# Where the nine sums of a source are written: PSUM layout, 16-bit words and GpSimd's copy in a graph kernel

## The chip, the cores and the metric

One core of one Trainium2 chip. The metric is the device time of one execution in microseconds; the kernel before takes 516.81 us (median of 3 runs, 516.4 to 516.84).

## The reference

6250 nodes with 64 features, 200,000 edges sorted by target, two graph convolutions behind a layer norm and a residual:

```python
def _ngcf_conv(x, W1, W2, src, dst, n_nodes):
    ones = jnp.ones(src.shape[0], dtype=x.dtype)
    deg_out = jnp.clip(jax.ops.segment_sum(ones, src, num_segments=n_nodes), 1.0)
    deg_in = jnp.clip(jax.ops.segment_sum(ones, dst, num_segments=n_nodes), 1.0)
    norm = jax.lax.rsqrt(deg_out[src] * deg_in[dst])
    h_src = x[src]
    h_dst = x[dst]
    msg = (h_src @ W1 + h_src * h_dst @ W2) * norm[:, None]
    agg = jax.ops.segment_sum(msg, dst, num_segments=n_nodes)
    return x @ W1 + agg

h = jnp.maximum(_layernorm(x, axis=-1), 0.0)
h1 = jax.nn.relu(_ngcf_conv(h, W1_1, W2_1, src, dst, n))
x = x + _ngcf_conv(h1, W1_2, W2_2, src, dst, n)
```

(n_nodes in the layer is 12500, but only the 6250 rows that occur are computed.)

## The kernel before

The kernel turns the edge list into a dense matrix of edge counts (targets by sources) on the chip, and then does both layers as dense matmuls with it. `fast_path` does all of it; a `general_path` behind it runs only where a flag says that the counts do not fit, which these inputs never need.

*Building the words.* Targets come in 49 blocks of 128, and each block in two units of 64 (98 units, `UNITS`). For a block VectorE writes one-hot rows `los` (`low_hots`, L663, a ring of three blocks), for a pair of steps TensorE multiplies `select` with the edges' digits into `diff` (`weigh_hots`, L879) and ScalarE turns that into weights `hots` (`save_weights`, L1025). Then `products(u)` (L895) runs 24 accumulated matmuls of 98 columns into one PSUM bank, `slab[u % 2]`. A bank holds nine rows of 49 sums: row 0 is the count of edges by source (for the out-degree), rows 1 to 8 are packed words, each with counts of eight targets in 2-bit fields. Each matmul adds 49 columns to row 0 and 49 columns to row `group + 1`.

*Saving them.* ScalarE's `save_words(u)` (L1034) copies the 441 sums to `saved` (a ring of two blocks), with 2^23 added so that the integer stands in the low bits. GpSimd's `keep_words(b)`, once per block, adds the histogram rows of both units to `hist` (L460) and copies the low 16 bits of the word rows, transposed, to `words[:, b]` (L463), 16 words for each of the 49 sources. The copy releases ScalarE's ring (`words_copied`) and VectorE's unpack of that block. GpSimd runs in order, and the same queue holds the indirect fetches of the edges, the decoding of later tiles (`decode`) and the layer norm (`moments`, `apply_norm`).

*Unpacking.* `unpack(n)` (L702 for the first field, L704 for the other three) takes the 400 32-bit words of a block and writes four fields as 8-bit floats, one block of the adjacency matrix, into one of five homes. Blocks 0, 1 and 2 are unpacked beside the building, behind the `los` of blocks 30, 34 and 38 (`UNPACK_BESIDE`), later ones three positions ahead of their use.

*The join.* After the last block VectorE adds the two histogram halves (L729) and the last block's two histogram rows out of PSUM (L732, L735), takes the root's reciprocal and scales h into `parts0` (L746, L753) in pieces, with which TensorE begins layer 1 (L966).

*The layers.* 98 positions (`POSITIONS`), 49 for each layer. Position n has 49 matmuls (L988), one per source block; between them, at fixed places, the transposition of a position before (`turn_pair`, L937, at q = 26, waits for VectorE's pair L781 and GpSimd's product L551) and its weight matmul (`weigh`, L955 or L959, at q = 43). VectorE's order in a position of layer 2 is: finish (L802), sums (L774), pair (L781), unpack (L702, L704 three times). The flag is made at position BLOCKS + 4 from two totals.

Of the kernel before, what the change touches and what calls it, by code (L numbers as in the profile page):

```python
# [19 lines left out]
P, Q = 125, 50  # L20
# [24 lines left out]
HOT_RING = 4  # L45
SAVED_RING = 2
EARLY_TILES = 4
# [4 lines left out]
BOTH = 1.0 + 0x3C / 1024.0  # L52
MAGIC = 2.0 ** 23
SC0 = 2.0 ** 12
# [58 lines left out]
def fast_path(nc, c, x, src, dst, weights, out, flag):  # L113
    def sb(name, shape, dt):
        return c.enter_context(nc.sbuf_tensor(name, shape, dt))
# [11 lines left out]

    words = sb("words", [128, BLOCKS, Q, WORDS], U16)
    x_sb = sb("x_sb", [128, BLOCKS, D], FP32)
# [3 lines left out]
    hots = sb("hots", [128, HOT_RING, USTEPS, Q - 1], FP16)  # L133
    saved = sb("saved", [128, SAVED_RING, 2, COLS], FP32)
    mixed = sb("mixed", [128, KEYLEN + STACKLEN], BF16)
# [9 lines left out]
    mask = sb("mask", [96, WORDS], FP32)  # L145
    hist = sb("hist", [128, 2, Q - 1], I32)
    last = sb("last", [SROWS, 1], FP32)
# [28 lines left out]
    rdo_sc0 = sb("rdo_sc0", [128, BLOCKS], FP32)  # L176
    totals = sb("totals", [128, 2], FP32)
    checks = sb("checks", [1, 2], FP32)
# [17 lines left out]
    junk = los_1[0:ROWS, 3 * GROUPS + 2 * WINDOW:3 * GROUPS + 2 * WINDOW + TILES * SAMPLES].rearrange("p (t e) -> p t e", t=TILES)  # L196
    words_late = flat_words[:, (BLOCKS - 3) * Q * WORDS:].bitcast(FP32)
    wabs = words_late[:, 448:512]
# [68 lines left out]
    weights_ready = sem("weights_ready")  # L267
    words_copied = sem("words_copied")
    hist_added = sem("hist_added")
# [103 lines left out]
    with nc.Block() as block:  # L373
# [52 lines left out]
        def _(pool):  # L426
# [19 lines left out]
                                    base=0, pattern=[[-1, 128]], channel_multiplier=1).then_inc(consts, 1)  # L446
            nc.gpsimd.memset(hist[:].bitcast(FP32), -(2.0 ** 97)).then_inc(hist_added, 1)
            nc.gpsimd.memset(words[:, :, Q - 1:Q, :], 0).then_inc(consts, 1)
# [5 lines left out]

            def keep_words(b):
                pool.wait_ge(slab_saved, 2 * b + 2)
                both = saved[:, b % SAVED_RING]
                if b < BLOCKS - 1:
                    pool.wait_ge(hist_added, b + 1)
                    nc.gpsimd.tensor_tensor(out=hist[:], in0=hist[:], in1=both[:, :, 0:Q - 1].bitcast(I32),  # L460
                                            op=ALU.add).then_inc(hist_added, 1)
                low = both[:, :, Q - 1:COLS].bitcast(U16).rearrange("p i (w q k) -> p q i w k", w=8, k=2)
                nc.gpsimd.tensor_scalar(words[:, b, 0:Q - 1, :].rearrange("p q (i w) -> p q i w", i=2), low[:, :, :, :, 0],  # L463
                                        1.0, 0.0, ALU.mult, ALU.add).then_inc(words_copied, 1)

# [62 lines left out]
            for u in range(UNITS):  # L528
                if u % 2 == 1:
                    keep_words(u // 2)  # L530
# [47 lines left out]
        def _(dve):  # L578
# [113 lines left out]
            def unpack(n, fields=range(4)):  # L692
                if n >= 5:
                    dve.wait_ge(acc_ready, n - 2)
                if n < BLOCKS:
                    dve.wait_ge(words_copied, n + 1)
                packed = words[:, n % BLOCKS].rearrange("p q w -> p (q w)").bitcast(I32).rearrange(
                    "p (q w) -> p q w", w=WORDS // 2)
                for s in fields:
                    to = tile_words[home(n)][:, :, 8 * s:8 * s + 8]  # L700
# [27 lines left out]
            dve.wait_ge(hist_added, BLOCKS)  # L728
            nc.vector.tensor_tensor(out=rdo[:], in0=hist[:, 0], in1=hist[:, 1], op=ALU.add).then_inc(deg_summed, 1)  # L729
            dve.wait_ge(deg_summed, 1)  # L730
            dve.wait_ge(slab_ready, UNITS - 1)
            nc.vector.tensor_tensor(out=degrees, in0=rdo[:], in1=slab[0][:, 0:Q - 1], op=ALU.add).then_inc(deg_summed, 1)  # L732
            dve.wait_ge(deg_summed, 2)
            dve.wait_ge(slab_ready, UNITS)
            nc.vector.tensor_tensor(out=degrees, in0=degrees, in1=slab[1][:, 0:Q - 1], op=ALU.add).then_inc(deg_summed, 1)  # L735
            dve.wait_ge(deg_summed, 3)
# [88 lines left out]
            for n in range(TOGETHER + 1, POSITIONS + 1):  # L825
                finish(n - 1)
                if n == BLOCKS:
                    dve.wait_ge(root_ready, BLOCKS)
                    nc.vector.tensor_reduce(out=totals[:, 1:2], in_=deg_in[:], axis=AX.X,
                                            op=ALU.add).then_inc(totals_ready, 1)  # L830
                if n == BLOCKS + 4:
                    dve.wait_ge(totals_summed, 1)
                    v(nc.vector.tensor_scalar(checks[:], sum_ps[0:1, 0:2], float(EDGES), None, ALU.is_equal))
                    v(nc.vector.tensor_tensor(out=flag[:], in0=checks[:, 0:1], in1=checks[:, 1:2], op=ALU.mult))
                if n < POSITIONS:
                    if n >= BLOCKS:
                        dve.wait_ge(z_used, min(n - BLOCKS + 1, BLOCKS))
                    sums(n)
                    if n + 3 < POSITIONS:
                        unpack(n + 3, (0, 1))  # L840
                    if n < BLOCKS:
                        low_turned(n)
                    if n + 3 < POSITIONS:
                        unpack(n + 3, (2, 3))

        @block.tensor
        def _(pe):
# [36 lines left out]
            def products(u):  # L884
# [86 lines left out]
            for n in range(TOGETHER, POSITIONS):  # L971
# [7 lines left out]
                for q in range(BLOCKS):  # L979
# [24 lines left out]
        def _(act):  # L1004
# [458 lines left out]
```

## Time and profile before

| | |
|---|---|
| median of the runs | 516.81 us |
| profiled execution, its own time | 518.48 us |
| its span | 516.8 us |
| TensorE busy | 485.1 us, 94% |
| VectorE busy | 410.2 us, 79% |
| ScalarE busy | 252.4 us, 49% |
| GpSimd busy | 220.9 us, 43% |

The span is what the profiler's records cover; the execution's own time is 1.7 us longer. Busy shares are averages over stages: about 25 us of start, the building of the words to 200 us, then two layers.

### The profile page before, as it was taken

How to read it: one execution, taken by the hardware profiler on the slowest of the kernel's cores; microseconds unless marked ns; L12 is line 12 of the kernel's file. 1: busy time of each engine (PE TensorE's matmuls, PEld its weight loads, DVE VectorE, ACT ScalarE, POOL GpSimd, SP SyncE). 2: the span in 40 equal slices, each digit the busy share in tenths (PEclk: the TensorE clock that was granted, in tenths of full speed). 3: DMA queues.
4: the chain of work that ended last, by engine and by line, in shares of the span. 5: the costliest groups of instructions: out<-in, count | busy, mean ns of one | idle time of the engine just before them, and what ended most of it. 6: DMA issues, size and time to landing. Idle time of an engine off the chain costs nothing.

```text
span 516.8 us, 19829 instructions
## 1 busy us (share of the span) xinstructions
PE 485.1 (94%) x7949; PEld 455.4 (88%) x7949; DVE 410.2 (79%) x1040; ACT 252.4 (49%) x726; POOL 220.9 (43%) x425
## 2 busy tenths in 40 slices
PE   2699999989997997999999999999999999999995
PEld 2577788878786887999999999999999999999995
DVE  6978999999999986987777777776766666666662
ACT  0279999999998795433333333333111121112111
POOL 3336879788999483453333433333100001100000
PEclk9879999999999898999999999999999999999998
DMA  2257102020201000000000000000000110020011
GB/s 68 82 95 94 47 21 64 3 63 3 65 1 43 2 3 1 3 4 2 3 4 3 3 3 2 3 4 3 3 1 3 21 26 1 3 44 1 3 29 20
DMA packets 17912, 10.89 MB, mean 21 GB/s; under 512 B 14144, under 2 KB 16496, under 8 KB 17821
## 3 DMA queue, kind: packets, MB, share of 16 engines
q1 hardware_dynamic: 17117, 7.60, 7.7%
q0 software_dynamic: 672, 2.01, 1.4%
q8 instruction: 64, 1.05, 0.8%
q14 instruction: 27, 0.22, 0.1%
q10 hardware_dynamic: 32, 0.01, 0.0%
HBM read 6.21 MB, written 3.33 MB: 18 GB/s over the span
## 4 chain that ended last, share of the span: by engine, by line
PE 72%; DVE 17%; issue 5%; ACT 2%; DMA 2%; POOL 1%; SPq 0%; DVEq 0%; ACTq 0%; POOLq 0%
PE diff L988 34%; PE iota_bank L988 17%; DVE los L663 9%; PE slab L895 8%; PE diff L879 4%; PE diff L959 2%; PE diff L966 1%; DVE stats L671 1%; ACT hots L1025 1%; PE slab L937 1%; DMA los<-in_dst_dram 1%; PE diff L955 1%; PE turn_t L937 1%; DVE rows L652 1%; DVE late L704 1%
## 5 line engine op out<-in xcount | busy, mean ns | idle before, releaser
L663 DVE TENSOR_TENSOR los<-mixed,iota_bank 128x5120 bf16<-128x5120 bf16 x49 | 136.3, 2810 | 7.0 <-PE slab L895 6.9
L895 PEld LDWEIGHTS slab<-hots,los 128*128 128x128 bf16 x2352 | 122.0, 99 | 17.5 <-issue 4.4
L895 PE MATMUL slab<-hots,los 128*128 128x98 fp8e5 x2352 | 128.2, 211 | 3.0 <-DVE los L663 2.9
L551 POOL TENSOR_TENSOR work<-work,h 128x64 f32<-128x64 f32 x98 | 31.4, 321 | 214.7 <-DVE work L774 214.7
L1025 ACT ACTIVATE hots<-diff 128x784 f16<-128x784 f32 x147 | 118.7, 847 | 9.1 <-PE diff L879 8.8
L988 PE MATMUL diff<-late,mixed 128*128 128x128 f16 x1616 | 104.4, 219 | 0.0
L988 PEld LDWEIGHTS diff<-late,mixed 128*128 128x128 fp8e4 x1616 | 98.7, 99 | 0.4
L988 PE MATMUL diff<-los,mixed 128*128 128x129 f16 x1470 | 95.7, 220 | 0.0
L988 PEld LDWEIGHTS diff<-los,mixed 128*128 128x128 fp8e4 x1470 | 89.3, 98 | 0.3
L463 POOL TENSOR_SCALAR words<-saved 128x784 uint16<-128x784 uint16 x49 | 79.2, 1617 | 7.8 <-ACT saved L1034 7.4
L879 PE MATMUL diff<-select,mixed 80*128 80x392 f16 x294 | 69.4, 342 | 8.4 <-ACT hots L1025 5.0
L704 DVE TENSOR_SCALAR mixed<-words 128x400 int32<-128x400 int32 x192 | 61.1, 359 | 0.0
L1034 ACT ACTIVATE saved<-slab 128x441 f32<-128x441 f32 x98 | 53.4, 545 | 10.6 <-PE slab L895 7.1
L988 PE MATMUL iota_bank<-late,tile 128*128 128x128 f16 x784 | 51.5, 219 | 0.0
L988 PE MATMUL iota_bank<-los,tile 128*128 128x129 f16 x735 | 49.0, 220 | 0.0
L988 PEld LDWEIGHTS iota_bank<-late,tile 128*128 128x128 fp8e4 x784 | 48.0, 98 | 0.2
L988 PEld LDWEIGHTS iota_bank<-los,tile 128*128 128x128 fp8e4 x735 | 45.0, 98 | 0.2
L781 DVE SCALAR_TENSOR_TENSOR work<-h,stats,work 128x64 f32<-128x64 f32 x98 | 39.5, 403 | 4.5
L879 PEld LDWEIGHTS diff<-select,mixed 80*128 80x128 f16 x294 | 23.6, 101 | 20.3 <-ACT hots L1025 10.2
L802 DVE SCALAR_TENSOR_TENSOR x_sb<-diff,stats,x_sb 128x64 f32<-128x64 f32 x49 | 13.9, 284 | 30.5 <-PE diff L959 30.5
L460 POOL TENSOR_TENSOR hist<-hist,saved 128x98 int32<-128x98 int32 x48 | 18.6, 387 | 39.6 <-ACT saved L1034 31.4
L704 DVE TENSOR_SCALAR tile<-words 128x400 int32<-128x400 int32 x96 | 32.7, 380 | 0.0
(172 smaller groups left out, 537.8 us busy)
## 6 DMA issues: line engine op xcount, KB each, us to landing
x_sb<-in_x_dram SPq DMA_DIRECT2D x4, 384.0 KB
rows_table<-rows SPq DMA_DIRECT2D x6, 252.0 KB
mixed<-rows_table SPq DMA_DIRECT2D x18, 84.0 KB
out_dram<-x_sb SPq DMA_DIRECT2D x8, 128.0 KB
los<-in_dst_dram SPq DMA_DIRECT2D x1, 750.0 KB
out_dram<-x_sb SPq DMA_DIRECT2D x4, 80.0 KB
out_dram<-x_sb SPq DMA_DIRECT2D x4, 48.0 KB
rows_table<-rows SPq DMA_DIRECT2D x1, 180.0 KB
```

The lines of the kernel that those rows point to most:

```text
L460: nc.gpsimd.tensor_tensor(out=hist[:], in0=hist[:], in1=both[:, :, 0:Q - 1].bitcast(I32), op=ALU.add).then_inc(hist_added, 1)
L463: nc.gpsimd.tensor_scalar(words[:, b, 0:Q - 1, :].rearrange("p q (i w) -> p q i w", i=2), low[:, :, :, :, 0], 1.0, 0.0, ALU.mult, ALU.add) ...
L551: nc.gpsimd.tensor_tensor(out=pair[a][:, 1], in0=s_sum[a], in1=h[:, b], op=ALU.mult).then_inc(product_ready, 1)
L663: nc.vector.tensor_tensor(out=los[:, b % LOS_RING].rearrange("e s (v t) -> e s v t", t=2), in0=key, in1=val, op=ALU.is_equal).then_inc(los ...
L704: ins = nc.vector.tensor_scalar(to, packed, 2 * s, 0x03030303, ALU.logical_shift_right, ALU.bitwise_and)
L781: nc.vector.scalar_tensor_tensor(pair[a][:, 0], h[:, b], root[:, b:b + 1], s_sum[a], ALU.mult, ALU.add).then_inc(pair_ready, 1)
L802: nc.vector.scalar_tensor_tensor(x_sb[:, b], turn_z[a][:, 0:D], rdi[:, b:b + 1], x_sb[:, b], ALU.mult, ALU.add).then_inc(y_ready, 1)
L879: ins = nc.tensor.matmul(diff[m % 2][:, bank, 0:HALF], stack[0:80, t % 2, j, k * 128:(k + 1) * 128], select[0:80, i * HALF:(i + 1) * HALF] ...
L895: ins = nc.tensor.matmul(to, los[:, u // 2 % LOS_RING, u % 2 * ULOWS + low], pairs, start=(step == 0), stop=(step == USTEPS - 1), skip_gro ...
L988: ins = nc.tensor.matmul(bank(n)[:, 0:width], tiles[home(n)][:, q], parts[:, q, 0:width], start=(q == 0), stop=(q == BLOCKS - 1))
L1025: nc.scalar.activation(bass.AP(to.tensor, to.offset, [to.ap[0], [step, 2], [STEPS * BLOCKS, 8], [1, BLOCKS]]), diff[m % 2][:, :, 0:HALF].r ...
L1034: nc.scalar.activation(saved[:, u // 2 % SAVED_RING, u % 2], slab[u % 2][:, 0:COLS], ACT.Copy, bias=MAGIC).then_inc(slab_saved, 1)
```

## The change

TensorE's matmul of L895 writes its columns nine PSUM words apart, so that a source's nine sums are neighbours; in even units the word rows stand in reverse order. ScalarE writes them straight into `words` as 16-bit integers, nine per source and unit. `words` has 18 slots per source instead of 16, the two histogram counts in slots 8 and 9, where they read as one 32-bit number; GpSimd adds these, and the ring `saved`, the copy and the semaphore `words_copied` are gone. VectorE's unpack reads two fours out of each nine 32-bit words. Since a 16-bit write could saturate, VectorE takes the largest of all words (48 maxima in layer 2), compares it with 65535 and reduces it; the flag is now made at the last position, and TensorE's matmul of the totals stands at q = 23 of the last position.

```diff
-SAVED_RING = 2
+SLOTS = 18
+FULL = 65535.0
-    words = sb("words", [128, BLOCKS, Q, WORDS], U16)
+    words = sb("words", [128, BLOCKS, Q, SLOTS], U16)
-    saved = sb("saved", [128, SAVED_RING, 2, COLS], FP32)
-    hist = sb("hist", [128, 2, Q - 1], I32)
+    hist = sb("hist", [128, Q - 1], I32)
+    largest = sb("largest", [128, Q * SLOTS], U16)
...
+    LARGEST_BESIDE = {BLOCKS + 3: (1, 2), BLOCKS + 4: (3, 4), BLOCKS + 5: (5, 6), **{BLOCKS + b - 1: (b,) for b in range(7, BLOCKS - 2)},
+                      POSITIONS - 3: (BLOCKS - 2, BLOCKS - 1)}
...
-            def keep_words(b):
+            def add_degrees(b):
                 pool.wait_ge(slab_saved, 2 * b + 2)
-                both = saved[:, b % SAVED_RING]
-                if b < BLOCKS - 1:
-                    pool.wait_ge(hist_added, b + 1)
-                    nc.gpsimd.tensor_tensor(out=hist[:], in0=hist[:], in1=both[:, :, 0:Q - 1].bitcast(I32),
-                                            op=ALU.add).then_inc(hist_added, 1)
-                low = both[:, :, Q - 1:COLS].bitcast(U16).rearrange("p i (w q k) -> p q i w k", w=8, k=2)
-                nc.gpsimd.tensor_scalar(words[:, b, 0:Q - 1, :].rearrange("p q (i w) -> p q i w", i=2), low[:, :, :, :, 0],
-                                        1.0, 0.0, ALU.mult, ALU.add).then_inc(words_copied, 1)
+                pool.wait_ge(hist_added, b + 1)
+                nc.gpsimd.tensor_tensor(out=hist[:], in0=hist[:],
+                                        in1=words[:, b, 0:Q - 1, WORDS // 2:WORDS // 2 + 2].bitcast(I32)[:, :, 0],
+                                        op=ALU.add).then_inc(hist_added, 1)
...
                 if n < BLOCKS:
-                    dve.wait_ge(words_copied, n + 1)
-                packed = words[:, n % BLOCKS].rearrange("p q w -> p (q w)").bitcast(I32).rearrange(
-                    "p (q w) -> p q w", w=WORDS // 2)
+                    dve.wait_ge(slab_saved, 2 * n + 2)
+                pairs = words[:, n % BLOCKS].rearrange("p q s -> p (q s)").bitcast(I32)
+                packed = bass.AP(pairs.tensor, pairs.offset,
+                                 [pairs.ap[0], [SLOTS // 2, Q], [SLOTS // 2 - WORDS // 4, 2], [1, WORDS // 4]])
...
-            nc.vector.tensor_tensor(out=rdo[:], in0=hist[:, 0], in1=hist[:, 1], op=ALU.add).then_inc(deg_summed, 1)
+            nc.vector.tensor_tensor(out=rdo[:], in0=hist_of[:, :, 0], in1=hist_of[:, :, 1], op=ALU.add).then_inc(deg_summed, 1)
...
-                if n == BLOCKS + 4:
-                    dve.wait_ge(totals_summed, 1)
-                    v(nc.vector.tensor_scalar(checks[:], sum_ps[0:1, 0:2], float(EDGES), None, ALU.is_equal))
-                    v(nc.vector.tensor_tensor(out=flag[:], in0=checks[:, 0:1], in1=checks[:, 1:2], op=ALU.mult))
...
+                for b in LARGEST_BESIDE.get(n, ()):
+                    if b > 1:
+                        dve.wait_ge(largest_taken, b - 1)
+                    nc.vector.tensor_tensor(out=largest[:], in0=largest[:] if b > 1 else flat_words[:, 0:Q * SLOTS],
+                                            in1=words[:, b].rearrange("p q s -> p (q s)"),
+                                            op=ALU.max).then_inc(largest_taken, 1)
+                if n == POSITIONS - 2:
+                    dve.wait_ge(largest_taken, BLOCKS - 1)
+                    v(nc.vector.tensor_scalar(largest[:], largest[:], FULL, None, ALU.is_ge))
+                    nc.vector.tensor_reduce(out=totals[:, 2:3], in_=largest[:], axis=AX.X,
+                                            op=ALU.max).then_inc(totals_ready, 1)
+                if n == POSITIONS - 1:
+                    dve.wait_ge(totals_summed, 1)
+                    v(nc.vector.tensor_scalar(checks[:, 0:2], sum_ps[0:1, 0:2], float(EDGES), None, ALU.is_equal))
+                    v(nc.vector.tensor_scalar(checks[:, 2:3], sum_ps[0:1, 2:3], 0.0, None, ALU.is_equal))
+                    v(nc.vector.tensor_tensor(out=checks[:, 0:1], in0=checks[:, 0:1], in1=checks[:, 1:2], op=ALU.mult))
+                    v(nc.vector.tensor_tensor(out=flag[:], in0=checks[:, 0:1], in1=checks[:, 2:3], op=ALU.mult))
...
-                    to = bass.AP(mine.tensor, mine.offset, [mine.ap[0], [(group + 1) * BLOCKS, 2], [1, BLOCKS]])
+                    place = 8 - group if u % 2 == 0 else group + 1
+                    to = bass.AP(mine.tensor, mine.offset, [mine.ap[0], [place, 2], [9, BLOCKS]])
...
-                    if n == BLOCKS + 2 and q == LATE:
-                        pe.wait_ge(totals_ready, 1)
-                        nc.tensor.matmul(sum_ps[0:1, 0:2], ones[:], totals[:], start=True,
+                    if n == POSITIONS - 1 and q == EARLY - 3:
+                        pe.wait_ge(totals_ready, 2)
+                        nc.tensor.matmul(sum_ps[0:1, 0:3], ones[:], totals[:], start=True,
                                          stop=True).then_inc(totals_summed, 1)
...
-                if u // 2 >= SAVED_RING:
-                    act.wait_ge(words_copied, u // 2 - SAVED_RING + 1)
-                    act.wait_ge(hist_added, u // 2 - SAVED_RING + 2)
-                nc.scalar.activation(saved[:, u // 2 % SAVED_RING, u % 2], slab[u % 2][:, 0:COLS], ACT.Copy,
-                                     bias=MAGIC).then_inc(slab_saved, 1)
+                mine = slab[u % 2][:]
+                first, step = (0, 1) if u % 2 else (8, -1)
+                nc.scalar.activation(words[:, u // 2, 0:Q - 1, 9 * (u % 2):9 * (u % 2) + 9],
+                                     bass.AP(mine.tensor, mine.offset + first, [mine.ap[0], [9, BLOCKS], [step, 9]]),
+                                     ACT.Copy).then_inc(slab_saved, 1)
```

## Rows read from the trace of the kernel before

**Rows 1.** The page: busy time by engine, and the chain's shares

```profile
PE 485.1 (94%) x7949; PEld 455.4 (88%) x7949; DVE 410.2 (79%) x1040; ACT 252.4 (49%) x726; POOL 220.9 (43%) x425
...
PE 72%; DVE 17%; issue 5%; ACT 2%; DMA 2%; POOL 1%; SPq 0%; DVEq 0%; ACTq 0%; POOLq 0%
...
L463 POOL TENSOR_SCALAR words<-saved 128x784 uint16<-128x784 uint16 x49 | 79.2, 1617 | 7.8 <-ACT saved L1034 7.4
```

**Rows 2.** Windows: length, busy PE, PEld, DVE, ACT, POOL, then granted clock, DMA share, GB/s

```profile
24.60:28.00 3.40, 3.40 (x29) 2.42 (x28) 3.37 (x4) 1.33 (x2) 0.00 (x0) 0.50 0.24 59
182.60:195.60 13.00, 13.00 (x218) 11.33 (x217) 10.87 (x4) 12.61 (x22) 9.49 (x10) 1.00 0.01 3
168.00:172.50 4.50, 4.45 (x52) 3.78 (x53) 4.50 (x2) 1.79 (x3) 0.00 (x0) 0.62 0.00 0
363.00:505.00 142.00, 142.00 (x2361) 141.33 (x2359) 96.90 (x324) 27.08 (x92) 14.44 (x46) 1.00 0.07 12
```

**Rows 3.** Chain of waits: start us, us, what; an early unit, and 182 us

```profile
24.76 2.06 PE slab L895 x24
...
182.75 1.12 PE slab L895 x24
...
185.99 1.12 PE slab L895 x24
```

**Rows 4.** Timeline, 158 to 182 us: start us, us, engine line, [idle before <-releaser]

```profile
160.27 1.57 POOL L463 TENSOR_SCALAR words<-saved 128x784 uint16<-128x784 uint16 x1
160.55 1.52 DVE L702 TENSOR_SCALAR tile<-words 128x400 int32<-128x400 int32 x1
161.99 3.19 DVE L704 TENSOR_SCALAR tile<-words 128x400 int32<-128x400 int32 x3
...
168.06 1.35 PE L895 MATMUL slab<-hots,los 128*128 128x98 fp8e5 x24 [2.89 <-DVE los L663]
```

**Rows 5.** Single lines: count, then min/median/max ns

```profile
L663 DVE TENSOR_TENSOR los<-mixed,iota_bank x49: 2762/2809/2822, 18.7 to 191.9; 128x5120 bf16<-128x5120 bf16 x49
L704 DVE TENSOR_SCALAR tile<-words x96: 352/356/1728, 162.0 to 496.7; 128x400 int32<-128x400 int32 x96
L650 DVE SCALAR_TENSOR_TENSOR p_rows_sb<-work,words x3: 1126/1131/1377, 103.6 to 152.5; 112x384 bf16<-112x384 int32 x3
L650 DVE SCALAR_TENSOR_TENSOR p_rows_sb<-work,late x2: 551/568/586, 52.8 to 78.2; 112x384 bf16<-112x384 int32 x2
```

**Rows 6.** Timeline around 153 us, TensorE

```profile
153.69 0.32 PE L865 MATMUL turn_t<-identb,p_rows_sb 112*128 112x112 bf16 x3 [0.62 <-DVE p_rows_sb L650]
```

**Rows 7.** Timeline of the join of building and layer 1

```profile
199.00 1.54 DVE L729 TENSOR_TENSOR rdo<-hist 128x49 f32<-128x49 int32 x1 [4.26 <-POOL hist L460]
200.81 0.21 DVE L735 TENSOR_TENSOR stats<-stats,slab 128x49 f32<-128x49 f32 x1
203.12 0.62 DVE L746 TENSOR_TENSOR los<-h,rdo_sc 128x448 f32<-128x448 f32 x1
```

**Rows 8.** ScalarE's two lines in the building, min/median/max ns

```profile
L1034 ACT ACTIVATE saved<-slab x98: 518/540/586, 30.0 to 207.3; 128x441 f32<-128x441 f32 x98
L1025 ACT ACTIVATE hots<-diff x147: 826/840/884, 23.0 to 196.2; 128x784 f16<-128x784 f32 x147
```

**Rows 9.** Timeline of one position of layer 2: VectorE, TensorE's turn

```profile
436.74 0.91 DVE L704 TENSOR_SCALAR mixed<-words 128x400 int32<-128x400 int32 x3
438.21 0.28 DVE L802 SCALAR_TENSOR_TENSOR x_sb<-diff,stats,x_sb 128x64 f32<-128x64 f32 x1 [0.57 <-PE diff L959]
438.90 0.28 DVE L774 SCALAR_TENSOR_TENSOR work<-iota_bank,unscale,work 128x64 f32<-128x64 f32 x1 [0.40 <-ACT work L1094]
439.78 0.14 PEld L937 LDWEIGHTS turn_t<-ident,work 128*128 128x128 f32 x1
```

**Rows 10.** Timeline of the end on VectorE

```profile
508.01 0.44 DVE L781 SCALAR_TENSOR_TENSOR work<-h,stats,work 128x64 f32<-128x64 f32 x1
512.80 0.28 DVE L802 SCALAR_TENSOR_TENSOR x_sb<-diff,stats,x_sb 128x64 f32<-128x64 f32 x1 [1.23 <-PE diff L959]
```

More of the change, by code:

```diff
@@ L52 @@
 BOTH = 1.0 + 0x3C / 1024.0
-MAGIC = 2.0 ** 23
 SC0 = 2.0 ** 12
@@ L176, in fast_path @@
     rdo_sc0 = sb("rdo_sc0", [128, BLOCKS], FP32)
-    totals = sb("totals", [128, 2], FP32)
-    checks = sb("checks", [1, 2], FP32)
+    totals = sb("totals", [128, 3], FP32)
+    checks = sb("checks", [1, 3], FP32)
     of_stats = stats[:].rearrange("p b s -> p (b s)")
     deg_in, root_in, root, rdi, rdi_rdo, degrees = [of_stats[:, i * BLOCKS:(i + 1) * BLOCKS] for i in range(6)]
-    flat_words = words[:].rearrange("p b q w -> p (b q w)")
+    flat_words = words[:].rearrange("p b q s -> p (b q s)")
     fine = []
     for t in range(TILES):
-        at = t * 4 * SPAN if t < EARLY_TILES else (BLOCKS - 9 + 2 * (t - EARLY_TILES)) * Q * WORDS
+        at = t * 4 * SPAN if t < EARLY_TILES else (BLOCKS - 9 + 2 * (t - EARLY_TILES)) * Q * SLOTS
         home = late if t < EARLY_TILES else flat_words
@@ L196, in fast_path @@
     junk = los_1[0:ROWS, 3 * GROUPS + 2 * WINDOW:3 * GROUPS + 2 * WINDOW + TILES * SAMPLES].rearrange("p (t e) -> p t e", t=TILES)
-    words_late = flat_words[:, (BLOCKS - 3) * Q * WORDS:].bitcast(FP32)
+    words_late = flat_words[:, (BLOCKS - 3) * Q * SLOTS:].bitcast(FP32)
     wabs = words_late[:, 448:512]
@@ L223, in fast_path @@
     halves_t = [work[:, (10 + 2 * i) * D:(12 + 2 * i) * D].bitcast(FP16).rearrange("p (k f) -> p k f", k=2) for i in range(2)]
+    hist_of = hist[:].bitcast(U16).rearrange("p (q i) -> p q i", i=2)
     rdi_h = spread[:, 0]
@@ L267, in fast_path @@
     weights_ready = sem("weights_ready")
-    words_copied = sem("words_copied")
     hist_added = sem("hist_added")
@@ L316, in fast_path @@
     totals_summed = sem("totals_summed")
+    largest_taken = sem("largest_taken")
     y_ready = sem("y_ready")
@@ L446, in _ @@
                                     base=0, pattern=[[-1, 128]], channel_multiplier=1).then_inc(consts, 1)
-            nc.gpsimd.memset(hist[:].bitcast(FP32), -(2.0 ** 97)).then_inc(hist_added, 1)
+            nc.gpsimd.memset(hist[:], 0).then_inc(hist_added, 1)
             nc.gpsimd.memset(words[:, :, Q - 1:Q, :], 0).then_inc(consts, 1)
@@ L528, in _ @@
             for u in range(UNITS):
-                if u % 2 == 1:
-                    keep_words(u // 2)
+                if u % 2 == 1 and u // 2 < BLOCKS - 1:
+                    add_degrees(u // 2)
                 if u in FETCH_AFTER:
@@ L695, in unpack @@
                 if n < BLOCKS:
-                    dve.wait_ge(words_copied, n + 1)
-                packed = words[:, n % BLOCKS].rearrange("p q w -> p (q w)").bitcast(I32).rearrange(
-                    "p (q w) -> p q w", w=WORDS // 2)
+                    dve.wait_ge(slab_saved, 2 * n + 2)
+                pairs = words[:, n % BLOCKS].rearrange("p q s -> p (q s)").bitcast(I32)
+                packed = bass.AP(pairs.tensor, pairs.offset,
+                                 [pairs.ap[0], [SLOTS // 2, Q], [SLOTS // 2 - WORDS // 4, 2], [1, WORDS // 4]])
                 for s in fields:
-                    to = tile_words[home(n)][:, :, 8 * s:8 * s + 8]
+                    to = tile_words[home(n)][:, :, 8 * s:8 * s + 8].rearrange("p q (i w) -> p q i w", i=2)
                     if s == 0:
@@ L728, in _ @@
             dve.wait_ge(hist_added, BLOCKS)
-            nc.vector.tensor_tensor(out=rdo[:], in0=hist[:, 0], in1=hist[:, 1], op=ALU.add).then_inc(deg_summed, 1)
+            nc.vector.tensor_tensor(out=rdo[:], in0=hist_of[:, :, 0], in1=hist_of[:, :, 1], op=ALU.add).then_inc(deg_summed, 1)
             dve.wait_ge(deg_summed, 1)
             dve.wait_ge(slab_ready, UNITS - 1)
-            nc.vector.tensor_tensor(out=degrees, in0=rdo[:], in1=slab[0][:, 0:Q - 1], op=ALU.add).then_inc(deg_summed, 1)
+            nc.vector.tensor_tensor(out=degrees, in0=rdo[:], in1=slab[0][:, 0:COLS:9], op=ALU.add).then_inc(deg_summed, 1)
             dve.wait_ge(deg_summed, 2)
             dve.wait_ge(slab_ready, UNITS)
-            nc.vector.tensor_tensor(out=degrees, in0=degrees, in1=slab[1][:, 0:Q - 1], op=ALU.add).then_inc(deg_summed, 1)
+            nc.vector.tensor_tensor(out=degrees, in0=degrees, in1=slab[1][:, 0:COLS:9], op=ALU.add).then_inc(deg_summed, 1)
             dve.wait_ge(deg_summed, 3)
```

## The prediction

> **What bounds the kernel now.** I read the page first [rows 1]: TensorE is busy 94% of the span and carries 72% of the chain of waits, VectorE 17%, GpSimd 1%. GpSimd's 220.9 us are therefore mostly work that nobody waits for, and 79.2 us of them are the copy that the change removes (49 x 1617 ns). The question is where its 1% and its side effects sit.
>
> I then read the stages [rows 2]. In the building of the words from 182.6 to 195.6 us TensorE is busy 13.00 of 13.00 us, ScalarE 12.61, VectorE 10.87, GpSimd 9.49. The reader is to see three nearly full engines, TensorE first. The chain there holds nothing but TensorE and repeats itself [rows 3]: twice 24 products in 1.12 us and six weight matmuls for the other 1.00, 3.24 us per block of 128 targets (182.75 to 185.99). In layer 2 TensorE is busy 142.00 of 142.00 us, VectorE 68%. So the kernel is TensorE's instruction stream plus its few stalls, and the change can gain only in those stalls and lose wherever it makes a TensorE instruction longer or later.
>
> The stalls come from the trace in time order. The big one is at 165.0 to 168.0 us [rows 2, 4]: TensorE waits 2.89 us for VectorE's `los` (L663), which could not start before 165.1, because unpack(2) before it took from 160.55 to 161.99 + 3.19. Its first instruction took 1.52 us and the next three 3.19 us, while GpSimd's copy (L463) of 1.57 us ran from 160.27 and the next one followed. Alone the same instruction takes 356 ns in the median [rows 5], three in a row 0.91 us [rows 9]. So VectorE's unpack stands still while GpSimd's copy runs. The same is seen at L650, 551 to 586 ns in two places and 1126 to 1377 ns in three [rows 5].
>
> **The change part by part.**
>
> *GpSimd's copy goes.* (a) The stall at blocks 39 and 40: unpack(2) then takes about 1.3 us, `los` 39 starts near 161.9 and ends near 164.7, before TensorE wants it at about 165.05. TensorE gets back 2.89 us and what the lower clock behind it cost: in 168.0 to 172.5 the granted clock averages 0.62 of 2.4 GHz, so 38% of 4.5 us, 1.7 us. Together 4.6. (b) L650 at 152.50: 1.13 us against 0.57; TensorE's turn waits 0.62 us for it and gets 0.56 back [rows 6]. The slowest L650, near 104 us, is 1377 - 568 = 0.8 us too long, but ScalarE loads a table and works beside it there, so I count nothing of it. (c) unpack(0) and unpack(1) are stretched in the same way; the ring of three blocks hides them but for an estimated 0.2 us. (d) The join to layer 1 [rows 7]: VectorE's sum of the histogram halves ran 1.54 us, from 199.00, behind the copy from 198.94, and its successor L735 started at 200.81. The last product ends at 200.20, so L735 could start at 200.25: 0.55. The copy of the last block stretches work of VectorE too, but TensorE is full there. Sum: 4.6 + 0.56 + 0.2 + 0.55 = 5.9 us. The bounds are 3 (the clock falls elsewhere) and 8.4 (0.8 more at 104 us, and a second spell of low clock, behind the join, gone too: 1.7 us, as in (a)).
>
> *TensorE's columns nine words apart.* The count of products does not change, 2352. Before, 98 sums went into two runs of 49 neighbouring words; now each lands nine words from the last. No product, weight or layer matmul of the trace writes in such steps, so the price is unknown. From below: 1.12/24 = 46.7 ns each, as now (a gain has no reason: 98 columns at 2.4 GHz are 40.8 ns). From above: the row at 24.76 us [rows 3], in which 24 products at 1.2 GHz (granted clock 0.50 [rows 2]) took 2.06 us, 86 ns each, the price if every column took two of the fast clock's periods. Two things lead me to the lower end. The second run of 49 begins at an odd word in half of the steps and at an even one in the others, and the mean stays within 5.9 ns of full rate; a port that took only aligned pairs would need some 74 half-rate periods at 1.2 GHz, 62 ns, in half of the steps, a mean of at least 52. And a step of nine alternates odd and even words. The nearest row is 46.7 ns; I take it. Each ns more costs 2.35 us over the kernel.
>
> *ScalarE writes 16-bit integers.* As many elements, 441, two per block. 784 elements into 16-bit floats take 840 ns, 441 into 32-bit 540 [rows 8]: 0.87 ns per element across both types, so the type costs nothing. Runs of nine, backwards in even units, have no row: 0 to +0.38 us each (441 steps of 0.87 ns doubled). I take 0, the rate of the two rows. The cover is thin: 0.39 us in 13, about 0.1 per block, 0.05 per instruction.
>
> *GpSimd's histogram sum* has 49 elements for 98 and stays hidden; behind GpSimd's queue (fetches, decoding, norm) nobody waits any more for words.
>
> *Unpack reads rows of nine 32-bit words, two fours of each.* 400 elements still. 354 ns lies below 400 cycles of one per cycle (1.04 ns each by L746's slope, an estimate from its 448 in 0.62 us less the 0.15 that any instruction costs [rows 7]), so two elements go at once. From below 354, from above 354 + 208 = 562 ns; I take 354 to 400. In layer 2 VectorE idles 0.57 us before L802 and 0.40 before L774 [rows 9], in which 4 x 0.05 disappears.
>
> *VectorE's 48 maxima over 900 16-bit words.* By L663 (5120 elements, 2809 ns, 0.55 each) 0.6 us; by L746 (1.04 each) 1.09 us. I take 0.6, both being 16-bit two-source instructions. In layer 2, VectorE's last unpack ends at 436.74 + 0.91 = 437.65; +0.2 +0.6 is 438.45, L802 then runs to 438.73, and L774 starts at 438.90 as before: hidden, with 0.17 us left. Where a position has two maxima (BLOCKS+3, +4, +5) 0.6 us does not fit: pair and product come late for the turn: L781 ends 0.76 us after L774 starts (0.32, and 0.44 of its own), at 439.66, and the turn starts at 439.78, 0.12 us of slack; about 0.9 us in all (0.3 to 1.6). The pair at POSITIONS-3 has no unpack beside it and is free.
>
> *The check at the end.* TensorE now waits at q = 23 of the last position for a threshold and a reduction over 900 words. It begins when the sums of position 96 are complete, which ScalarE and then VectorE take up (L774, L781), an estimated 0.95 us before L781 starts at 508.01 [rows 10], so near 507.05; q = 23 comes at 507.05 + 23 x 0.057 = 508.4. VectorE's sums(96) end at 508.45 [rows 10]; then the threshold (0.35 to 1.09, I take 0.5), the reduction (900 x 1.04 + 0.14 = 1.08) and two handovers of 0.1: 510.2. TensorE stands 1.8 us (1.4 to 2.5), and behind it in its queue are the rest of position 97, turn and weigh of 96, the last turn and the last store: all of it on the path. VectorE's four small checks fit into the 1.23 us before the last L802 [rows 10].
>
> Sum: -5.9 + 0.9 + 1.8 = -3.2 us. The profiled execution took 518.48 us with a span of 516.8, the median of the runs is 516.81; 518.48 - 3.2 is 515.3, and against the median 513.6.
>
> **The rivals.**
>
> R1, the strided write is dear. Each step costs a slot of two columns, 86 ns for 46.7: 0.94 us per unit, 98 units, 92 us; the remaining waits for the other engines (another 3 us) vanish under it. 516.8 + 92 - 5.9 - 3 + 2.7 = 602.6 us. It decides from 1.4 ns per product, where 3.2 us are gone. For it: no row shows such a write. Against it: the insensitivity to odd starts. Chance 0.29.
>
> The Trainium skill, page "PSUM — Partial Sum Buffer", section "Specifications (TRN2)", says that PSUM's lines are 8 bytes and that "any non-contiguous AP slows matmuls significantly"; it gives no figure, and no run here shows it yet. By that rule R1 is what happens.
>
> R2, ScalarE becomes the pace. At +0.15 us per instruction a block grows by 0.3 - 0.1 = 0.2 us, 46 blocks: +9, 523 us. For: only 0.1 us of slack. Against: its rate is the same for 16-bit writes. 0.09.
>
> R3, VectorE becomes the pace of layer 2. The maximum at 1.09 us ends at 438.94, L802 at 439.2, L774 starts 0.3 us late; with 0.12 of slack 0.2 per position, 43 positions: +9, 522.6 us. 0.07.
>
> R4, costs eat the gain: only 3 to 4 us come back and the end costs 2.5: 516.5 us, no change. 0.08.
>
> **How the numbers follow.** The forecast, faster by 3.2 us, has 0.47. Its own range is 511 to 515.6. A measurement tells about 0.2%, 1.0 us, from no change. Faster: 0.47 and a little of R4, 0.48; same 0.09; slower 0.43 (R1 to R3, which leave the forecast by the wrong side). The range goes from 510.8 to 604: R1 alone holds more than the 0.2 that may stay outside, so it has to be taken in.
>
> **What would show it.** Right: L895 24 in 1.12 us and 3.24 us per block; no 2.9 us stall near 165; unpack never over 0.45 us; ScalarE's save at 0.54; the maximum near 0.6; one TensorE stall of 1.5 to 2 us at the matmul of the totals. Wrong: 24 products in over 1.2 us, which alone turns the sign; or ScalarE at 100% with TensorE waiting for its slab; or TensorE waiting for L781 throughout layer 2.

## The result and the profile after

The changed kernel takes 594.85 us (median of 4 runs, 593.97 to 594.93) against 516.83 (the kernel before, median of 4): ratio 1.1496, 95% interval [1.1473, 1.1519]. It is 78 us slower. The forecast of 513.6 us is wrong in its sign; the time lies where rival R1 stood (602.6 us), inside the range.

The page of the changed kernel, the lines that answer to [rows 1], TensorE's products and ScalarE's save:

```profile
PE 566.3 (96%) x7949; PEld 541.8 (92%) x7949; DVE 425.8 (72%) x1092; ACT 260.7 (44%) x726; POOL 138.4 (23%) x376
...
PE 94%; DVE 3%; DMA 1%; ACT 1%; issue 0%; SPq 0%; DVEq 0%
...
L914 PE MATMUL slab<-hots,los 128*128 128x98 fp8e5 x2352 | 215.3, 286 | 0.1
...
L1052 ACT ACTIVATE words<-slab 128x441 uint16<-128x441 f32 x98 | 58.7, 599 | 75.5 <-PE slab L914 75.4
```

The same number of matmuls, 7949, is busy 81 us longer, and the chain of waits is TensorE for 94% instead of 72%. GpSimd's 82 us less are seen nowhere in the time. ScalarE's save now waits 75 us for TensorE, against 7.1 before. The chain in the building (start us, us, what) says how much longer each unit is:

```profile
205.88 2.02 PE slab L914 x24
207.90 0.33 PE diff L896 x2
208.24 2.02 PE slab L914 x24
210.26 0.15 PE turn_t L882 x3
```

24 products took 1.12 us [rows 3] and now 2.02 us: 84.2 ns each for 46.7. The weight matmuls between them, whose output is still one run, are unchanged at 0.33 us for two. The granted clock in this stretch is 1.00. In the first unit it is 0.50 for the first 18 of the 24 products, which together take 3.58 us for the 2.06 of [rows 3] (the chain's row, then a window of 9 products: length, busy PE, PEld, DVE, ACT, POOL, granted clock, DMA share, GB/s):

```profile
24.69 3.58 PE slab L914 x24
24.69:25.90 1.21, 1.21 (x9) 1.21 (x9) 1.21 (x1) 0.82 (x1) 0.00 (x0) 0.50 0.26 57
```

From start to start a product takes 160 to 166 ns at this clock, where the kernel before took 80 to 85. The step doubles the product at either clock. Everything else of the change lies close to the prediction, as VectorE's lines show (single lines: count, min/median/max ns; then the end's timeline):

```profile
L848 DVE TENSOR_TENSOR largest<-largest,words x47: 612/615/630, 446.0 to 579.4; 128x900 uint16<-128x900 uint16 x47
```

```profile
582.34 1.09 DVE L854 TENSOR_REDUCE totals<-largest 128x1 f32<-128x900 uint16 x1
583.49 0.19 PE L1015 MATMUL slab<-totals,ones 128*1 128x3 f32 x2 [1.32 <-DVE totals L854]
```

### The profile page after: what moved, and what is told of

Its sections match the earlier page's. It is cut to its first block, busy times and chain, and to the rows that moved or that the text cites. A ratio compares the mean times of both kernels' runs of the same rounds, so it can differ in the third digit from the quotient of the medians.

```text
span 592.1 us, 19739 instructions
## 1 busy us (share of the span) xinstructions
PE 566.3 (96%) x7949; PEld 541.8 (92%) x7949; DVE 425.8 (72%) x1092; ACT 260.7 (44%) x726; POOL 138.4 (23%) x376
## 4 chain that ended last, share of the span: by engine, by line
PE 94%; DVE 3%; DMA 1%; ACT 1%; issue 0%; SPq 0%; DVEq 0%
PE slab L914 34%; PE diff L1007 30%; PE iota_bank L1007 15%; PE diff L896 8%; PE diff L978 2%; PE diff L985 1%; PE slab L956 1%; DMA los<-in_dst_dram 1%; PE turn_t L956 1%; PE diff L974 1%; ACT hots L1044 1%; PE iota_bank L985 1%; PE slab L1007 0%; DMA mixed<-rows 0%; PE diff L871 0%
## 5 line engine op out<-in xcount | busy, mean ns | idle before, releaser
L914 PE MATMUL slab<-hots,los 128*128 128x98 fp8e5 x2352 | 215.3, 286 | 0.1
L914 PEld LDWEIGHTS slab<-hots,los 128*128 128x128 bf16 x2352 | 202.2, 134 | 13.4 <-ACT hots L1044 0.6
L666 DVE TENSOR_TENSOR los<-mixed,iota_bank 128x5120 bf16<-128x5120 bf16 x49 | 138.0, 2820 | 84.8 <-PE slab L914 84.8
L1044 ACT ACTIVATE hots<-diff 128x784 f16<-128x784 f32 x147 | 116.5, 833 | 8.5 <-PE diff L896 8.5
L1052 ACT ACTIVATE words<-slab 128x441 uint16<-128x441 f32 x98 | 58.7, 599 | 75.5 <-PE slab L914 75.4
L465 POOL TENSOR_TENSOR hist<-hist,words 128x49 int32<-128x49 int32 x48 | 14.9, 311 | 192.2 <-ACT words L1052 153.7
L896 PEld LDWEIGHTS diff<-select,mixed 80*128 80x128 f16 x294 | 30.3, 121 | 13.0 <-issue 3.7
L708 DVE TENSOR_SCALAR tile<-words 128x400 int32<-128x400 int32 x96 | 30.4, 357 | 0.0
L848 DVE TENSOR_TENSOR largest<-largest,words 128x900 uint16<-128x900 uint16 x47 | 29.0, 616 | 0.1
L1113 ACT ACTIVATE work<-diff,unscale 128x64 f32<-128x64 f32 x33 | 10.3, 313 | 38.1 <-PE diff L1007 37.1
```

Source lines behind the costliest of these rows:

```text
L465: nc.gpsimd.tensor_tensor(out=hist[:], in0=hist[:], in1=words[:, b, 0:Q - 1, WORDS // 2:WORDS // 2 + 2].bitcast(I32)[:, :, 0], op=ALU.add) ...
L666: nc.vector.tensor_tensor(out=los[:, b % LOS_RING].rearrange("e s (v t) -> e s v t", t=2), in0=key, in1=val, op=ALU.is_equal).then_inc(los ...
L848: nc.vector.tensor_tensor(out=largest[:], in0=largest[:] if b > 1 else flat_words[:, 0:Q * SLOTS], in1=words[:, b].rearrange("p q s -> p ( ...
L896: ins = nc.tensor.matmul(diff[m % 2][:, bank, 0:HALF], stack[0:80, t % 2, j, k * 128:(k + 1) * 128], select[0:80, i * HALF:(i + 1) * HALF] ...
L914: ins = nc.tensor.matmul(to, los[:, u // 2 % LOS_RING, u % 2 * ULOWS + low], pairs, start=(step == 0), stop=(step == USTEPS - 1), skip_gro ...
L1044: nc.scalar.activation(bass.AP(to.tensor, to.offset, [to.ap[0], [step, 2], [STEPS * BLOCKS, 8], [1, BLOCKS]]), diff[m % 2][:, :, 0:HALF].r ...
```

## The experiments

Two questions: is it TensorE's step of nine words alone, and what about the step is dear? Then the side that the prediction counted as gain: where does it come from, and can it be had without the loss?

**e1_rows.** The change with TensorE's rows back:

```diff
-to = bass.AP(mine.tensor, mine.offset, [mine.ap[0], [place, 2], [9, BLOCKS]])
+to = bass.AP(mine.tensor, mine.offset, [mine.ap[0], [place * BLOCKS, 2], [1, BLOCKS]])
-bass.AP(mine.tensor, mine.offset + first, [mine.ap[0], [9, BLOCKS], [step, 9]])
+bass.AP(mine.tensor, mine.offset + first * BLOCKS, [mine.ap[0], [1, BLOCKS], [step * BLOCKS, 9]])
...
```

(VectorE's two reads of the last histogram rows out of PSUM follow the rows back, here and in e2, e6, e7, e8 and e9.)

> The changed kernel with one part undone: TensorE writes its two runs of 49 neighbouring words again (rows of 49 in the bank), and ScalarE gathers a source's nine sums with a step of 49 words while it writes the same 16-bit words. Theory A (all of the loss is TensorE's step of nine words): 24 products in 1.12 us instead of 2.02, 84 ns back to 47, and the kernel at about 513 to 516 us, since the end's wait (1.3 us) and the maxima stay and GpSimd's copy stays away. Theory B (other parts of the change, ScalarE's dearer writes or VectorE's maxima, carry part of the loss): products at 47 ns and yet over 525 us. Open besides: if ScalarE's read with a step of 49 words costs as TensorE's step does, its 600 ns become some 900 and ScalarE sets the pace of a block at about 3.9 us, 545 us in all.

514.31 us, ratio to the kernel before 0.9942 [0.9921, 0.9963]. The chain of e1 in the building:

```profile
180.65 1.12 PE slab L914 x24
...
183.89 1.12 PE slab L914 x24
```

The products are back at 46.7 ns and a block at 3.24 us. Theory A holds. One access pattern is worth 80.5 us (594.85 - 514.31; 78.7 between the two profiled executions), and without it the change is faster than the kernel before by 2.6 us, 0.6%. ScalarE's read with a step of 49 words is free: 603 ns in the median against 600 where a source's nine sums are neighbours.

**e2_rows_scatter.** TensorE as in e1; ScalarE reads each row in order and scatters on the write.

```diff
+nc.scalar.activation(words[:, u // 2, 0:Q - 1, 9 * (u % 2):9 * (u % 2) + 9].rearrange("p q s -> p s q"),
+    bass.AP(mine.tensor, mine.offset + first * BLOCKS, [mine.ap[0], [step * BLOCKS, 9], [1, BLOCKS]]), ...
```

> As e1_rows, but ScalarE reads the rows of 49 neighbouring words in order and scatters on the write: each 16-bit integer lands 36 bytes from the last. Theory A: TensorE at 47 ns again whatever ScalarE does. On ScalarE: if its writes of single 16-bit elements are as free as runs, 540 to 600 ns and 513 to 516 us; if single elements far apart cost a second period each, about 900 ns, ScalarE is the pace and the kernel takes about 545 us. The comparison with e1_rows tells whether a step is dearer on ScalarE's read or on its write.

643.51 us, ratio 1.2435 [1.2413, 1.2458]. The single line of ScalarE's save:

```profile
L1052 ACT ACTIVATE words<-slab x98: 2041/2164/2745, 29.8 to 330.6; 128x441 uint16<-128x441 f32 x98
```

TensorE's products stayed at 47 ns from start to start (median), so theory A holds on its side. On ScalarE both of my values failed, 600 and 900 ns: 2164 ns for 441 elements is 4.9 ns each, 3.6 times what runs of nine took (603 in all). In 100 to 120 us ScalarE is busy 20.00 of 20.00 us and sets the pace; its other line, the hots, rose too, to 1156 ns in the mean.

**e3_before_step9.** The kernel before with only TensorE's step; ScalarE gathers with a step of nine into the old rows.

```diff
-[mine.ap[0], [(group + 1) * BLOCKS, 2], [1, BLOCKS]]
+[mine.ap[0], [group + 1, 2], [9, BLOCKS]]
...
-saved[...], slab[u % 2][:, 0:COLS]
+saved[...].rearrange("p (r q) -> p r q", r=9), slab[u % 2][:, 0:COLS].rearrange("p (q r) -> p r q", r=9)
```

> The kernel before with one part of the change alone: TensorE writes its columns nine words apart, ScalarE gathers them with a step of nine into the old rows; GpSimd's copy, the old words, the old check all stay. Theory A: the products alone take 84 ns each and the kernel 594 to 600 us: 98 units x 0.90 us is 88 us, less the stalls of 6 to 8 us that vanish under a slower TensorE. Theory B (the slowness needs the change's other parts, for example ScalarE's reads of the bank or writes): products near 47 ns, or clearly under 580 us.

593.3 us, ratio 1.1462 [1.1436, 1.1489]. The step alone, with none of the rest, makes 76 of the 78 us; the time is 0.7 us under the lower end that I had given. The changed kernel is 1.5 us slower still, though it has no copy on GpSimd: the copy's absence gains nothing under the slow step, and the wait at the end costs its 1.3 us. ScalarE's save took 539 ns reading with a step of nine and writing 32-bit neighbours, 540 before [rows 8], so the 60 ns that the changed kernel pays are not the read's: they come with the write, 16-bit integers in runs of nine. Type and runs are not told apart.

**e4_patterns and e5_lines.** The kernel before, with groups of 24 matmuls behind its last one. Only the output pattern differs within 98-column groups:

```diff
+for i in range(24):
+    nc.tensor.matmul(bass.AP(mine.tensor, mine.offset + off, [mine.ap[0]] + pattern), los[:, 0, i], moving, start=(i == 0), ...)
```

> The kernel before with 16 groups of 24 matmuls behind its last one, each group with 98 columns (96 in one) and the same weights and moving data, and another output pattern: one run, two runs of 49 (second at an even and at an odd word), steps of 2, 3, 4, 5 words, two interleaved steps of 9 and of 10, aligned pairs, pairs from an odd word, pairs nine words apart, runs of three and of seven, backwards, and step 9 without accumulation. Reads the price of the pattern itself. Theory A1 (a word that does not share an aligned pair of words with its predecessor costs a second period, whatever the step): runs and aligned pairs 47 ns, all steps 84, pairs from an odd word 84, runs of seven and three between. Theory A2 (even and odd words are separate, so an odd step is cheap and an even one dear): would have step 3, 5 and 9 at 47 and 2, 4, 10 at 84; the changed kernel speaks against it already. Theory A3 (it is the reading back of the sum for the accumulation): step 9 without accumulation at 47. The whole takes some 25 to 35 us longer.

> As e4_patterns, with 150 matmuls ahead so that the clock is at 2.4 GHz in all groups (in e4 it was not in the first three). Law drawn from e4's groups: a matmul takes about 4 ns and one period of 1.2 GHz (0.83 ns) for every aligned pair of words that its columns touch one after another. It expects run98 even 49 pairs, 43 to 45 ns; run98 odd 50, 45; two runs of 49 with an even or odd second start 50, 46; step 9 forwards or backwards 98, 84; runs of seven, even or odd start, four pairs each, 56, 50; runs of fourteen 49, 44; pairs ten words apart 49, 45; 49 columns in step 9 49 pairs, 44; 49 neighbouring columns 25 pairs, so the floor of a matmul, below 44. Rival (each step away costs a fixed time for the hop): runs_of_seven with odd start as with even start, but 49 columns in step 9 would need more than 98 neighbouring ones, and pairs ten apart more than run98.

The timeline on TensorE gives the start of each group. A group's first matmul still pays for the pattern of the one ahead of it, so the difference of two groups' starts over 24 is off by up to 2 ns (45.0 for L1026, 82.5 for L1028, 64.2 for L1030). The table has the mean distance from start to start inside each group, from its second matmul on. In e4 L1016 is a step of 3 words, L1018 of 4, L1020 of 5, L1022 two steps of 9, L1024 two of 10, L1026 aligned pairs, L1028 pairs from an odd word, L1030 pairs nine words apart, L1032 runs of seven, L1034 one run backwards:

```profile
519.92 2.22 PE L1016 MATMUL diff<-hots,los 128*128 128x98 fp8e5 x24
521.94 2.22 PE L1018 MATMUL diff<-hots,los 128*128 128x98 fp8e5 x24
523.96 2.22 PE L1020 MATMUL diff<-hots,los 128*128 128x98 fp8e5 x24
525.98 2.22 PE L1022 MATMUL diff<-hots,los 128*128 128x98 fp8e5 x24
528.00 2.22 PE L1024 MATMUL diff<-hots,los 128*128 128x98 fp8e5 x24
530.02 1.24 PE L1026 MATMUL diff<-hots,los 128*128 128x98 fp8e5 x24
531.10 2.18 PE L1028 MATMUL diff<-hots,los 128*128 128x98 fp8e5 x24
533.08 1.73 PE L1030 MATMUL diff<-hots,los 128*128 128x98 fp8e5 x24
534.62 1.38 PE L1032 MATMUL diff<-hots,los 128*128 128x98 fp8e5 x24
535.84 1.21 PE L1034 MATMUL diff<-hots,los 128*128 128x98 fp8e5 x24
```

In e5 L1014 and L1016 are two runs of 49, the second at an even and at an odd word, L1018 step 9 with 98 columns, L1022 step 9 with 49, L1024 49 neighbours, L1030 and L1032 runs of seven from even and from odd words:

```profile
520.89 1.24 PE L1014 MATMUL diff<-hots,los 128*128 128x98 fp8e5 x24
521.97 1.24 PE L1016 MATMUL diff<-hots,los 128*128 128x98 fp8e5 x24
523.05 2.18 PE L1018 MATMUL diff<-hots,los 128*128 128x98 fp8e5 x24
525.03 2.22 PE L1020 MATMUL diff<-hots,los 128*128 128x98 fp8e5 x24
527.05 1.24 PE L1022 MATMUL diff<-hots,los 128*128 128x49 fp8e5 x24
528.11 0.78 PE L1024 MATMUL diff<-hots,los 128*128 128x49 fp8e5 x24
...
529.93 1.36 PE L1030 MATMUL diff<-hots,los 128*128 128x98 fp8e5 x24
531.12 1.49 PE L1032 MATMUL diff<-hots,los 128*128 128x98 fp8e5 x24
532.44 1.22 PE L1034 MATMUL diff<-hots,los 128*128 128x98 fp8e5 x24
```

| pattern (98 columns, where not said) | aligned pairs touched | ns per matmul | pairs x 0.833 + 2.5 |
|---|---|---|---|
| one run from an even word (e5), backwards (e4) | 49 | 43.4, 43.4 | 43.3 |
| one run from an odd word (e5) | 50 | 44.2 | 44.2 |
| two runs of 49, second start even or odd (e5) | 50 | 45.0, 45.0 | 44.2 |
| pairs from even words, four apart (e4), ten apart (e5) | 49 | 43.4, 43.3 | 43.3 |
| runs of fourteen (e5) | 49 | 43.3 | 43.3 |
| runs of seven from even words (e4, e5) | 56 | 50.0, 49.9 | 49.2 |
| runs of seven from odd words (e5) | 56 | 55.0 | 49.2 |
| runs of three, 96 columns (e4) | 64 | 56.7 | 55.8 |
| pairs nine apart, so 24 of the 49 straddling (e4) | 73 | 63.4 | 63.3 |
| pairs from odd words (e4) | 98 | 84.2 | 84.2 |
| steps of 2, 3, 4, 5, 9, 10 (e4), 9 backwards (e5) | 98 | 84.1 to 84.2 | 84.2 |
| step 9, not accumulated (e4, e5) | 98 | 84.1, 84.1 | 84.2 |
| step 9, 49 columns (e5) | 49 | 43.4 | 43.3 |
| run of 49 columns (e5) | 25 | 25.0 | 23.3 |
| 24 columns, step 9 or one run (e5) | 24, 12 | 25.0, 25.0 | 22.5, 12.5 |

The reader is to see that the second column sets the third. The last column is fitted to these rows: 0.833 ns for each aligned pair of words that the columns touch in turn, plus 2.5 ns. At the granted clock of 1.00, 2.4 GHz, 0.833 ns is two periods; at 0.50, 1.2 GHz, the changed kernel's 98 pairs took about 163 ns, 1.67 each, two periods again. The law meets all rows within 1 ns but the shortest, where no matmul took less than 25.0 ns, and one: runs of seven from odd words took 55.0 ns where it says 49. Their 14 odd starts cost something more that I can't name.

A1 holds. A2 falls: steps of 3, 5 and 9 cost as much as 4 and 10. A3 falls: step 9 costs the same without accumulation. The rival of a fixed price per hop falls with the pairs. Pairs ten words apart, nine apart and four apart from odd words all have 48 hops, and took 43.3, 63.4 and 84.2 ns. The other test that I had named for it, 49 columns in step 9, decides nothing: a hop would cost 0.42 ns (84.2 less 43.3, over 97 hops), and 23.3 ns for 49 columns with 48 such hops make 43.5, as much as the law says. Each of e4 and e5 ran once. The first three groups of e4 ran partly at the lower clock and are not used; e5 has their patterns again.

The Trainium skill, page "PSUM — Partial Sum Buffer", section "Specifications (TRN2)", has lines of 8 bytes and the sentence that any non-contiguous pattern slows matmuls significantly. These rows agree on the line and give the size, 1.8 times in this kernel. They limit "any": pairs from even words, four or ten words apart, have a gap behind every second column and cost what one run does, 43.4 and 43.3 ns.

**e7_copy_back and e8_copy_as_before.** e1 with a GpSimd copy of 784 elements per block put back, whose result nobody reads; in e7 from neighbouring 16-bit elements, in e8 in the old form (every second element, transposed). From e8's lines:

```diff
...
+low = both[:, :, 0:16 * (Q - 1)].rearrange("p i (w q k) -> p q i w k", w=8, k=2)
+p(nc.gpsimd.tensor_scalar(spare[:].rearrange("p q (i w) -> p q i w", i=2), low[:, :, :, :, 0], 1.0, 0.0, ALU.mult, ALU.add))
```

> e1_rows with a GpSimd copy of 784 16-bit elements per block put back, from words into a spare tile that nobody reads, so that only its presence counts. Theory G (what the change gains is that GpSimd's copy no longer holds up VectorE's unpack): the stall of about 3 us at block 39 with its spell of low clock comes back, unpack 1.0 to 1.5 us an instruction beside the copy, 518 to 520 us. Rival S (it gains because ScalarE and VectorE wait for fewer semaphores and the ring is gone): stays at 514 to 515 us.

> e7's copy took 847 ns and not the 1617 of the kernel before, because it read and wrote 16-bit neighbours; the stall did not come back. Here the copy has the old form: it reads every second 16-bit element, transposed, out of the words of the two last blocks, into a spare tile. Theory G (what counts is how long GpSimd holds VectorE up): 1.6 us a copy, unpack(2) again over 3 us, the stall of 2.9 us and the low clock at block 39 back, 518 to 520 us. Rival S: the copy alone does nothing, and the gain over the kernel before came from the ring and the waits that are gone: 514 us.

e7 took 513.9 us, 0.9943 [0.9921, 0.9964]: no loss; its copy was a mere 847 ns. e8 took 518.62 us, 1.0017 [1.0005, 1.003], 4.3 us more than e1 in the medians and 3.6 between the profiled spans (517.0 and 513.4). e7's copy, then the timeline of e8:

```profile
L470 POOL TENSOR_SCALAR spare<-words x48: 838/847/1151, 31.8 to 192.3; 128x784 uint16<-128x784 uint16 x48
...
160.73 1.48 DVE L712 TENSOR_SCALAR tile<-words 128x400 int32<-128x400 int32 x1
...
162.14 2.38 DVE L714 TENSOR_SCALAR tile<-words 128x400 int32<-128x400 int32 x3
162.63 1.67 POOL L472 TENSOR_SCALAR spare<-words 128x784 uint16<-128x784 uint16 x1
...
167.40 1.28 PE L920 MATMUL slab<-hots,los 128*128 128x98 fp8e5 x24 [2.00 <-DVE los L672]
```

That is [rows 4] again, 2.00 us of wait for 2.89, though the ring and its waits are gone. In e1 the same unpack is short:

```profile
156.72 0.36 DVE L706 TENSOR_SCALAR tile<-words 128x400 int32<-128x400 int32 x1
156.99 0.91 DVE L708 TENSOR_SCALAR tile<-words 128x400 int32<-128x400 int32 x3
```

Theory G holds for the stall, with a condition: the copy has to be long and to fall on unpack(2). In e7 unpack(2) was not hit (no instruction over 364 ns there), only the first two were, up to 1151 ns, and TensorE has no wait for `los` in the building. What G had said of the clock did not come: e8's granted clock is 1.00 from 165 to 175 us, where the kernel before fell to 0.62 behind its stall [rows 2]. The 3.6 us are made up otherwise: the last product ends 3.1 us later than in e1 (2.00 of them this stall, 0.54 TensorE's wait for L659, the former L650), and the wait at the join is 3.21 us for 2.64.

**e6_late_totals and e9_no_maxima.** e1 with the matmul of the totals moved behind the last position's matmuls, and then without the 48 maxima (the check for overflow is left out).

```diff
-                    if n == POSITIONS - 1 and q == EARLY - 3:
-                        pe.wait_ge(totals_ready, 2)
-                        nc.tensor.matmul(sum_ps[0:1, 0:3], ones[:], totals[:], start=True,
-                                         stop=True).then_inc(totals_summed, 1)
...
+            pe.wait_ge(totals_ready, 2)
+            nc.tensor.matmul(sum_ps[0:1, 0:3], ones[:], totals[:], start=True,
+                             stop=True).then_inc(totals_summed, 1)
             turn_pair(POSITIONS - 1)
```

> e1_rows with TensorE's matmul of the totals moved behind the last position's 49 matmuls, ahead of the last turn, where TensorE waits for VectorE anyway. The end's wait of 1.3 us goes: e1 stands at 514.3, so 513.0 us, and no TensorE idle in front of the totals' matmul. Rival: the chip's last stores or the last turn set the end, or the checks then delay VectorE's last instruction, and nothing is gained.

> e6_late_totals without the 48 maxima; the threshold and the reduction stay, but look at the first block's words alone, so the check for 16-bit overflow is left out. If the maxima are hidden in VectorE's idle time, as TensorE's 133.00 busy of 133.00 us in layer 2 of e6 says: the same 511.8 us within 0.3. If three positions with two maxima cost what the prediction gave them: 0.9 us less, 510.9.

e6 took 511.76 us (510.27 to 512.61), 0.9886 [0.9867, 0.9905], 2.5 us under e1 in the medians. The wait of 1.32 us is gone and so is the matmul ahead of the turn: by the two traces e6 gains 1.6 us there. It was already 1.0 us ahead at layer 1's first transposition, which the edit does not touch, so 1.6 us is what the edit is worth. e9 took 512.1, 0.989 [0.9871, 0.9909], no less than e6. A loss of 0.9 us would hardly stand out from runs that spread over 2 us, but the traces tell it: from one transposition to the next e6 takes 3.17 us at most at the doubled positions and e9 3.13, and over the whole of layer 2 e6 loses 0.1 us to e9. The maxima cost next to nothing. e6's window of layer 2 (busy us of TensorE, its weight load, VectorE):

```profile
370.00:503.00 133.00, 133.00 (x2215) 132.48 (x2213) 113.12 (x340) 25.06 (x86) 13.75 (x43) 1.00 0.06 13
```

VectorE rose from 68% to 85% there and TensorE is still busy all of the time. e6 beats both kernels: 5.2 us (1.1%) under the kernel before, 83 under the changed one.

## Why the prediction was wrong

*The step that failed* is "The nearest row is 46.7 ns; I take it" under TensorE's columns. It measured 84.2 ns; the upper end given was 86. The reason given for the lower end was that a port which took only aligned pairs would need 74 periods, a mean of at least 52 ns, in the old layout. That reckoned with pairs fixed by the count of columns, first and second, third and fourth. e5 shows that they are not: a run that begins at an odd word spends one slot on its first column and then goes on in aligned pairs, 44.2 ns for a run of 98 from an odd word and 43.4 from an even one, 45.0 for two runs of 49 with either start. So the flat 46.7 ns excluded one way of pairing and said nothing about words that have no neighbour at all. The second reason, that a step of nine alternates odd and even words, is worth nothing: the steps of 3, 5 and 9 alternate and cost what 4 and 10 do, which keep to even words or change parity once.

*R1* had the mechanism and was 7.8 us too high. By e1, 2352 x 37.5 ns is 88.2 us. From block 3 to block 47 e1 takes 149.6 us where 44 x 3.24 are 142.6, the changed kernel 222.9 where 44 x 5.04 are 221.8: 5.9 us of e1's waits are covered. The first three blocks cost 3.2 us more and not 5.4, 2.2 less; there the granted clock was low for longer in e1 (0.62 from 28 to 34 us, 1.00 in the changed kernel). 80.1 of the 88.2 remain by this, and the last product ends 79.8 us later. The 7.8 us too many are three: 86 ns per product for 84.2 (3.8), costs of 2.7 us for 1.3 (1.4), and 2.6 us more of the old waits vanished than the 5.9 + 3 that I had reckoned.

*GpSimd's copy goes*: right in e1, where the step is undone. The last product ends at 200.20 us before and at 194.87 in e1, and the wait at the join shrank from 3.15 to 2.64:

```profile
203.35 1.83 PE L966 MATMUL diff<-los,late 128*128 128x129 f16 x14 [3.15 <-DVE los L753]
197.51 0.51 PE L985 MATMUL diff<-los,late 128*128 128x129 f16 x6 [2.64 <-DVE los L757]
```

Layer 1 begins 5.8 us earlier, for the predicted 5.9. e8 shows the cause for the stall, L650 and the join; the 1.6 us of low clock behind the stall (block 39 took 4.79 us, 3.24 in e1) are gone in e1, but e8 did not bring them back. Under the slow step this gain vanished: e3, which has the copy, is no slower than the changed kernel, and TensorE has no wait for `los` in its building either.

*ScalarE*: 600 ns for the expected 540. That is over the cover of 0.05 us that I named, and yet e1's block stayed at 3.24 us. *Unpack*: 356 ns, unchanged, at the lower end. *Maxima*: 615 ns each as taken; the 0.9 us for the doubled positions was wrong, 0.1 measured. *The check at the end*: 1.32 us for 1.8. R2, R3 and R4 did not occur. Without the step, the sum was -3.2 us; e1 measured -2.6. That the two are close is partly luck: the costs came to about 1.4 us for 2.7, and in e1's trace 0.9 of the 5.8 us are lost again between the start of layer 1 and its first transposition (12.22 us for 11.37), for a reason that stays open.

## What to carry to other kernels

When TensorE is the bound, count the aligned pairs of PSUM words that a matmul's columns touch in turn, not the columns (below some 27 pairs the 25 ns of the shortest matmuls ruled here): gather on the reading side, where a step of 49 words cost ScalarE nothing. On ScalarE's write keep small elements in runs. And a cost for which the trace has no row is bounded, not argued to one end: when one of the two ends changes the sign and the pattern can be timed by itself, time it first.

## What the runs showed that I had not expected

ScalarE's write of single 16-bit elements 36 bytes apart: 4.9 ns each, against 1.4 in runs of nine. A GpSimd copy of 784 16-bit elements takes 847 ns from neighbours and 1570 ns from every second one, transposed (medians). A run written backwards costs what one forwards does (43.4 ns in e4, 43.4 in e5). And no matmul was under 25.0 ns: 24 columns in one run or in step 9 took the same.
